# Five changes of order in the second half of a fused two-layer kernel

## The chip, the cores and the metric

The kernel runs on one core of one Trainium2 chip. The metric is the device time of one execution in microseconds (us); the number given for a kernel is the median of its runs. TensorE is also called PE, VectorE DVE, ScalarE ACT, GpSimd POOL and SyncE SP; PEld is TensorE's loading of weights.

## The reference

Two layers act on 2048 tokens of width 128, in float32. Layer 0 is a scan followed by attention and a soft mixture of 8 experts; it takes about the first 950 us and the change does not touch it. Layer 1, cut to what matters here:

```python
xn = layernorm(x)
# recurrent branch
h   = rmsnorm(xn) * w_norm
u, z = split(h @ W_in.T);  u = silu(u)              # 256 + 256 columns
lam = sigmoid(u @ W_dt.T + b_dt)
s_t = lam_t * s_(t-1) + (1 - lam_t) * u_t           # scan over the 2048 tokens
s   = xn + (s * silu(z)) @ W_out.T
# sparse experts: 16 experts, the best 2 of each token
w   = top2(softmax(xn @ Wr + br)), rescaled to sum 1
y_e = layernorm((silu(xn @ W1[e]) * (xn @ W3[e])) @ W2[e]) * gamma[e] + beta[e]
x   = x + s * silu(sum over the 2 experts of w * y_e)
```

## The kernel before, in words

Each engine has its own program, written out by hand; engines meet only in semaphores (`wait_ge`, `then_inc`), and each engine runs its program strictly in the written order. Tokens lie in 16 tiles of 128 rows (`T`), and in 4 chunks of 4 tiles (`C`, 512 tokens each; `LATE` is the last chunk).

**From layer 0 to the router.** VectorE makes the third layernorm chunk by chunk: `third_stats` gives the variance, ScalarE takes its root (`root(3, c)`), `third_apply` writes `xn2`. ScalarE scales the tiles for the RMS norm (`scale_tiles2`, L915), in one run of 12 tiles for the first three chunks, with the last chunk's root after the eighth of them. TensorE transposes both (`turn_norm` for `xn2`, `turn_scaled` for the scaled tiles), each chunk when its four tiles are there, and makes the router's logits. VectorE subtracts the row maximum (L1315), ScalarE takes the exponential (L941) and VectorE finds the two best experts and writes `mask` (L1335). ScalarE loads a table of functions ahead of an operation that needs another than the one in place (`ACT_TABLE_LOAD`); copies and plain scalings run under any table.

**From the mask to the slots.** TensorE counts the mask (`count`, L1888), makes W (the second half of u, L1876), then eight products M of 512 tokens each for `lam` (the step sizes, L1901), then R (`find_slots`, L1915: 32 small products that say which token stands in which slot), then eight products Z. The results go round the eight PSUM banks in the order of `SECOND_MM`. VectorE meanwhile writes R's inputs (`in_tile`, `of_tile`) and names each tile's expert (`name_experts`); then `place_tokens` reads R and writes `token` and `dest`, the rows that POOL's indirect transfers use. After it VectorE runs the scan, `recur(0)` and `recur(1)`; `recur` waits for all eight M.

**The tiles of the experts.** The 4096 token-expert pairs, sorted by expert, fill up to 47 tiles (`NT`) of 128 slots. For tile n:

- POOL gathers its rows (`gather_slots`, L699), up to 4 tiles ahead; SP loads its expert's weights, also up to 4 ahead (512 KB each, L598).
- TensorE transposes the rows (`turn_slots`, L1946), ScalarE copies them out (`copy_slots`, L965); one PSUM bank (`XB`) serves all, so a tile's transpose waits for the copy of the one before.
- TensorE makes the hidden products (`hidden_slots`, L1955), ScalarE their SiLU (`gate_slots`, L971), VectorE the product (`multiply`, L1433), TensorE the output (`outputs`, L1965). `hidden_slots(n)` waits for `multiply(n - 2)`.
- VectorE takes the output with its statistics (`take_output`).

The three first tiles are transposed ahead of the first hidden product, and in the loop tile n + 3 is turned in step n. During steps 2 to 5 TensorE also makes the recurrent branch's output (`states_out`, L1934).

**The groups.** `GROUPS` puts the tiles into eleven groups of four (the last is 40 to 43), then 44 and 45, then 46. After a group's last tile ScalarE takes the roots of its variances (`roots`, L976) and VectorE finishes the group (`finish_outputs`: a reciprocal and one product for each tile, L1461), on which POOL's scatters wait (`scatter_outputs`, L706, one transfer for each tile). `LAG` says how many steps after its last tile a group's roots come; `finish_outputs` came one step later still. When all 47 tiles are scattered, SP and ACT load the rows back (L478), and the rest is elementwise.

Of the kernel before, what the change touches and what calls it, by code (L numbers as in the profile page):

```python
# [42 lines left out]

NT = (2 * N + (P - 1) * E1) // P
GROUPS = [*(range(i, i + 4) for i in range(0, NT - 3, 4)), range(NT - 3, NT - 1), range(NT - 1, NT)]
LAG = [2] * (len(GROUPS) - 4) + [1] * 2 + [0] * 2
XT, RING = 4, 16
INNER = 2 * P

# [25 lines left out]
ROWS_W = _at  # L75
W_IN = 2 * F1
W_RING = 4
PICK = 32


# [59 lines left out]
def build(nc, x, mats, cols, rows, b2, gains, pick, tri, ones, w1, w2, w_in, w_out, out):  # L140
    with ExitStack() as ctx:
# [133 lines left out]
        def row(name):  # L275
# [150 lines left out]
        SECOND_BANK = Steps(A=C, L=1, B=C, U=C, K=1, W=C, M=2 * C, R=1, Z=2 * C)  # L426
        SECOND_MM = Order(("A", 0), ("A", 1), ("A", 2), ("B", 0), ("B", 1), ("A", 3), ("B", 2), ("L", 0),
                          ("U", 0), ("U", 1), ("U", 2), ("B", 3), ("U", 3), ("K", 0), *(("W", c) for c in range(C)),
                          *(("M", i) for i in range(2 * C)), ("R", 0), *(("Z", i) for i in range(2 * C)),
                          *(("Y", c) for c in range(C)))  # L430
        SECOND_ACT = Steps(A=C, B=C, U=C, W=C, M=2 * C, Z=2 * C)
        SECOND_DVE = Steps(L=1, K=1, R=1, Y=C)
# [287 lines left out]
        def _(act):  # L720
# [206 lines left out]
            silu_sum(LATE)  # L927
            act.wait_ge(norm3, LATE * TC)
            act.wait_ge(rms_inv, 1)
            scale_tiles2(0, 2 * TC)  # L930
            root(3, LATE)
            scale_tiles2(2 * TC, LATE * TC)
            copy_turned2(LATE)
            root_means(1)
            for c in range(LATE):
                gain_turned2(c)
            act.wait_ge(norm3, T)
            act.wait_ge(rms_inv, 2)
            scale_tiles2(LATE * TC, T)
            act.wait_ge(route_exp, 1)  # L940
            nc.scalar.activation(rp[:, :, :], rp[:, :, :], ACT.Exp).then_inc(route_exp, 1)  # L941
            gain_turned2(LATE)
            for j in range(2):
                for c in range(C):
# [30 lines left out]
                at = slice(GROUPS[i][0] % RING, GROUPS[i][-1] % RING + 1)  # L975
                nc.scalar.activation(y_rstd[:, at], y_rstd[:, at], ACT.Sqrt).then_inc(y_std, 1)  # L976

            for n in range(3):
                copy_slots(n)
            gate_slots(0)  # L980
            for n in range(NT):
                if n + 1 < NT:
                    gate_slots(n + 1)
                if n + 3 < NT:
                    copy_slots(n + 3)
                for i, group in enumerate(GROUPS):
                    if n == min(group[-1] + max(LAG[i], 1), NT - 1):
                        roots(i)
            nc.scalar.activation(table_set[:, :], table_set[:, :], ACT.Silu)
            act.wait_ge(s_gated, C)  # L990
# [19 lines left out]
        def _(dve):  # L1010
# [460 lines left out]
            for n in range(NT):  # L1471
                if 3 <= n < 3 + C:
                    take_states(n - 3)
                if n + 1 < NT:
                    multiply(n + 1)
                if n > 0:
                    take_output(n - 1)
                if n < C:
                    gate_states(n)
                if n == 3 + C:  # L1480
                    dve.wait_ge(second_dve, SECOND_DVE.n("Y"))
                    dve.nop().then_inc(s_gated, C)
                for i, group in enumerate(GROUPS):
                    if n == group[-1] + LAG[i] + 1:
                        finish_outputs(i)
            take_output(NT - 1)
            finish_outputs(len(GROUPS) - 1)
# [25 lines left out]
        def _(pe):  # L1513
# [327 lines left out]
            def fill_second(step, c, mms):  # L1841
                mms(second_bank(step, c)).then_inc(second_mm, 1)
# [49 lines left out]
            for c in range(C):  # L1892
                if c == C - 1:
                    pe.wait_ge(second_act, SECOND_ACT.n("U", 0))
                fill_second("W", c, from_h(1, c))
            for j in range(2):
                for c in range(C):
                    def mms(bank):
                        for i in range(2):
                            at = (i * 2 + j) * P  # L1900
                            last = pe.matmul(bank, mat("wdt")[:, at:at + P], u[i][:, c * CH:(c + 1) * CH],  # L1901
                                             start=(i == 0), stop=(i == 1))
                        return last
                    i = j * C + c
                    if j == 0:
                        pe.wait_ge(second_act, SECOND_ACT.n("W", c))
                    if i == C - 1:
                        pe.wait_ge(second_dve, SECOND_DVE.n("K"))
                    fill_second("M", i, mms)
            def find_slots(bank):  # L1910
                for k in range(2):
                    pe.wait_ge(in_tile_set, k + 1)
                    pe.wait_ge(of_tile_set, k + 1)
                    for t in range(T):
                        last = pe.matmul(bank[:, 0:2 * NT], in_tile[:, k, t, :], of_tile[k][:, t, :],  # L1915
                                         start=(k == 0 and t == 0), stop=(k == 1 and t == T - 1))
                return last
            pe.wait_ge(second_act, SECOND_ACT.n("M", 0))
            fill_second("R", 0, find_slots)
            for j in range(2):  # L1920
                for c in range(C):
                    i = j * C + c
# [47 lines left out]
            pe.wait_ge(second_act, SECOND_ACT.total)  # L1970
            pe.wait_ge(te_set, 1)
            pe.wait_ge(wall_in, 32)
            for n in range(3):
                turn_slots(n)
            hidden_slots(0)
            for n in range(NT):
                if n + 1 < NT:
                    hidden_slots(n + 1)
                if n > 0:
                    outputs(n - 1)  # L1980
                if 2 <= n < 2 + C:
                    states_out(n - 2)
                if n + 3 < NT:
                    turn_slots(n + 3)
            outputs(NT - 1)


# [65 lines left out]
```

## Time and profile before

| | us |
|---|---|
| Median of 3 runs | 1188.43 |
| Lowest and highest run | 1186.72, 1189.18 |
| The profiled execution | 1186.79 |
| Its span, first to last instruction | 1184.9 |
| PE, DVE, ACT, POOL busy | 1101.9, 909.5, 815.4, 346.9 |

The profile is of one execution; all times of day below are us from its span's start. Between 948 and 1014 us the engines hand work to each other one step at a time; from there to 1148 us TensorE works on the tiles without a pause; the rest is the end.

### The profile page before, as it was taken

What the parts mean: (1) busy time and instruction counts of PE and PEld (TensorE: products, weight loads), DVE (VectorE), ACT (ScalarE), POOL (GpSimd) and SP (SyncE); (2) the same over time, 40 slices, a digit from 0 to 9 for tenths busy, and PEclk for the clock granted to TensorE, in tenths of its full rate; (3) what the DMA queues carried; (4) which work ended last, traced back from release to release, by engine and by line L of the source; (5) the groups of instructions that cost most, each with busy time, mean ns of one, the idle gap of its engine ahead of it and who ended that gap; (6) DMA issues with size and microseconds to landing.
All of it is one profiled execution on the core that took longest, in us unless ns stands there. A gap on an engine that the chain in (4) does not pass through costs nothing.

```text
span 1184.9 us, 19441 instructions
## 1 busy us (share of the span) xinstructions
PE 1101.9 (93%) x6337; PEld 447.5 (38%) x6337; DVE 909.5 (77%) x1413; ACT 815.4 (69%) x1512; POOL 346.9 (29%) x852
## 2 busy tenths in 40 slices
PE   5979999999999999999999999999999979899990
PEld 2412222222222222222222244444444444799990
DVE  3689999999999999999999954433334878756664
ACT  2668888888888888888888864433334565255553
POOL 0476653234222242222322212000000001556752
PEclk9879999999999999999999999999999979899995
DMA  3313321032200322100201026000000001467754
GB/s 113 139 32 80 89 73 53 29 94 51 55 29 29 87 59 51 42 29 29 69 30 39 29 73 263 9 27 19 18 18 18 19 19 66 137 196 241 231 162 122
DMA packets 65496, 87.87 MB, mean 74 GB/s; under 512 B 28579, under 2 KB 39819, under 8 KB 64883
## 3 DMA queue, kind: packets, MB, share of 16 engines
q1 hardware_dynamic: 52434, 70.94, 18.8%
q0 software_dynamic: 10208, 13.45, 4.9%
q10 hardware_dynamic: 2758, 2.28, 0.7%
q8 instruction: 51, 0.84, 0.3%
q14 instruction: 45, 0.36, 0.1%
HBM read 60.83 MB, written 25.76 MB: 73 GB/s over the span
## 4 chain that ended last, share of the span: by engine, by line
PE 39%; issue 33%; POOL 20%; DVE 3%; ACT 2%; DMA 1%; POOLq 0%; DVEq 0%; ACTq 0%; SPq 0%
PE PS L1764 9%; PE PS L1754 9%; PE PS L1955 7%; POOL neg_m L640 6%; POOL big L453 4%; PE PS L1965 3%; POOL big L471 2%; PE PS L1901 1%; DVE mx L1076 1%; PE PS L1529 1%; POOL m_rest L646 1%; POOL m_cols L645 1%; POOL m_cols L647 1%; POOL m_rest L648 1%; POOL m_cols L649 1%
## 5 line engine op out<-in xcount | busy, mean ns | idle before, releaser
L1076 DVE TENSOR_REDUCE mx<-PS 128x1 f32<-128x1024 f32 x512 | 594.1, 1212 | 19.6 <-PE PS L1601 9.1
L1616 PE MATMUL PS<-big 59*128 59x512 bf16 x1024 | 294.6, 387 | 9.1 <-DMA big<-m_dram 2.4
L1601 PE MATMUL PS<-big 56*128 56x512 bf16 x1024 | 201.8, 385 | 16.6 <-DVE mx L1076 8.7
L811 ACT ACTIVATE xn<-PS 128x512 f32<-128x512 f32 x340 | 185.7, 604 | 27.4 <-PE PS L1616 27.4
L811 ACT ACTIVATE ctx_sb<-PS 128x512 f32<-128x512 f32 x344 | 187.8, 604 | 23.8 <-PE PS L1616 23.7
L811 ACT ACTIVATE xnT<-PS 128x512 f32<-128x512 f32 x340 | 185.6, 605 | 21.6 <-PE PS L1616 21.6
L1616 PEld LDWEIGHTS PS<-big 59*128 59x128 bf16 x1024 | 72.6, 94 | 325.5 <-ACT ctx_sb L811 98.6
L640 POOL TENSOR_SCALAR neg_m<-mx 128x1 f32<-128x1 f32 x256 | 68.9, 288 | 372.0 <-DVE mx L1076 372.0
L1206 DVE TENSOR_TENSOR ctx_sb<-big,PS 128x512 f32<-128x512 f32 x128 | 87.8, 686 | 116.4 <-PE PS L1764 70.4
L863 ACT ACTIVATE big<-PS,col_sb 128x512 f32<-128x512 f32 x128 | 87.8, 687 | 123.2 <-PE PS L1754 113.1
L699 POOL DMA_INDIRECT late<-xn_dram,gate_p x47 | 54.0, 1150 | 315.8 <-DVE gate_p L1407 277.2
L1754 PE MATMUL PS<-big,w_bufs 128*128 128x512 f32 x256 | 133.3, 603 | 0.1
L1764 PE MATMUL PS<-ctx_sb,w_bufs 128*128 128x512 f32 x256 | 131.8, 596 | 1.3 <-DVE ctx_sb L1206 1.3
L1601 PEld LDWEIGHTS PS<-big 56*128 56x128 bf16 x1024 | 50.4, 94 | 118.4 <-DVE mx L1076 114.0
L1955 PE MATMUL PS<-big 128*128 128x128 f32 x752 | 93.1, 278 | 0.0
L1628 PE MATMUL PS<-ctx_sb,v_cols 128*32 128x512 f32 x688 | 92.5, 610 | 0.0
L1628 PE MATMUL PS<-xnT,v_cols 128*32 128x512 f32 x680 | 91.2, 609 | 0.0
L1628 PE MATMUL PS<-xn,v_cols 128*32 128x512 f32 x680 | 90.6, 605 | 0.0
L1955 PEld LDWEIGHTS PS<-big 128*128 128x128 f32 x752 | 89.4, 195 | 0.0
L1764 PEld LDWEIGHTS PS<-ctx_sb,w_bufs 128*128 128x128 f32 x256 | 48.5, 191 | 64.0 <-issue 58.4
L1754 PEld LDWEIGHTS PS<-big,w_bufs 128*128 128x128 f32 x256 | 48.5, 192 | 53.9 <-issue 52.1
L1433 DVE TENSOR_TENSOR v_cols<-v_cols,PS 128x512 f32<-128x512 f32 x47 | 32.1, 683 | 40.8 <-ACT v_cols L971 40.8
(250 smaller groups left out, 1031.4 us busy)
## 6 DMA issues: line engine op xcount, KB each, us to landing
big<-in_w_in SPq DMA_DIRECT2D x47, 512.0 KB, 3.8
o_dram<-o_sum SPq DMA_DIRECT2D x64, 256.0 KB, 2.4
big<-parts_dram POOLq DMA_DIRECT2D x42, 128.0 KB, 4.6
w_bufs<-in_w SPq DMA_DIRECT2D x16, 256.0 KB, 2.6
big<-in_w_out SPq DMA_DIRECT2D x2, 2048.0 KB, 10.8
w_bufs<-o_dram SPq DMA_DIRECT2D x3, 1024.0 KB, 5.1
big<-parts_dram SPq DMA_DIRECT2D x62, 48.0 KB
big<-m_dram SPq DMA_DIRECT2D x128, 3.0 KB
```

Of the source, the lines that this page charges most:

```text
L640: ch.did(nc.gpsimd.tensor_scalar(m[:, u:u + 1], mx[:, b % 2, 2 * u:2 * u + 1], mx[:, b % 2, 2 * u + 1:2 * u + 2], -1.0, ALU.max, ALU.mult))
L699: pool.indirect_dma_start(xt[:, n % XT, :], None, xn_dram[:, :], bass.IndirectOffsetOnAxis(ap=token[:, n:n + 1], axis=0))\
L811: nc.scalar.activation(probs[i % SLOTS][:, r, :], PS[:, SB + n % SLOTS, :], ACT.Exp, scale=DH ** -0.5).then_inc(exp_done, 1)
L863: nc.scalar.activation(h_relu[:, f % 2, :], PS[:, HB + f % 2, :], ACT.Relu, bias=col_sb[:, bass.ds(COLS["b1"][0] + e * FT + f, 1)]).then_i ...
L1076: v.tensor_reduce(mx[:, b % 2, 2 * u + half:2 * u + half + 1], PS[:, MB + 2 * half:MB + 2 * half + 2, :].rearrange("p b n -> p (b n)"), AX ...
L1206: v.tensor_tensor(h_wt[:, f, :], h_relu[:, f % 2, :], PS[:, PB + slot, :], ALU.mult)\
L1601: mm = pe.matmul(PS[:, MB + 2 * half + k, :], q_all[rows_of, h, t * P:(t + 1) * P], k_all[rows_of, h, half * CH:(half + 1) * CH], start=Tr ...
L1616: pe.matmul(PS[:, SB + n % SLOTS, :], k_all[rows_of, h, at:at + P], q_all[rows_of, h, qc * CH:(qc + 1) * CH], start=True, stop=True).then_ ...
L1628: mm = pe.matmul(PS[VW * r:VW * (r + 1), PVB, :], v_cols[:, at:at + VW], probs[i % SLOTS][:, r, :], start=(s == 0), stop=(s == TC - 1))
L1754: pe.matmul(PS[:, HB + f % 2, :], w1_buf[:, par, f * P:(f + 1) * P], x1T[:, c * CH:(c + 1) * CH], start=True, stop=True).then_inc(h_mm, 1)
L1764: pe.matmul(PS[:, c, :], w2_buf[:, par, f * P:(f + 1) * P], h_wt[:, f, :], start=(isinstance(e, int) and e == 0 and f == 0), stop=last and ...
L1955: mm = pe.matmul(PS[:, b + n % 2, f:f + P], w_ring[:, n % W_RING, w + f:w + f + P], xtT[:, n % 4, :], start=True, stop=True)
```

## The change

- *Last groups' finish.* `finish_outputs` is placed by a list of its own. For all groups but one the step stays as it was; the group of tiles 40 to 43 is finished in step 44 instead of 45, right after `take_output(43)` and ahead of `multiply(45 + 1)`. The roots on ScalarE stay where they were.
- *First tile's inner products.* Only tile 0 is transposed ahead of `hidden_slots(0)`; tile 1 comes behind it, tile 2 in step 0, tile 3 in step 1, tiles 4 and 5 in step 2, and from step 3 on tile n + 3 as before. ScalarE's copies follow the same order.
- *Slot products ahead of the last step sizes.* R stands between the seventh and the eighth M.
- *Third norm's root.* ScalarE takes the last chunk's root after four scaled tiles instead of eight.
- *Router's exponential.* ScalarE takes it ahead of the last chunk's four scalings instead of behind them.

```diff
-LAG = [2] * (len(GROUPS) - 4) + [1] * 2 + [0] * 2
+LAG = [2] * (len(GROUPS) - 4) + [1] * 4
+FINISH = [3] * (len(GROUPS) - 4) + [2] + [1] * 3
+TURNS = [(2,), (3,), (4, 5), *((n + 3,) if n + 3 < NT else () for n in range(3, NT))]
...
-                          *(("M", i) for i in range(2 * C)), ("R", 0), *(("Z", i) for i in range(2 * C)),
+                          *(("M", i) for i in range(2 * C - 1)), ("R", 0), ("M", 2 * C - 1),
+                          *(("Z", i) for i in range(2 * C)),
...
-            scale_tiles2(0, 2 * TC)
+            scale_tiles2(0, TC)
             root(3, LATE)
-            scale_tiles2(2 * TC, LATE * TC)
+            scale_tiles2(TC, LATE * TC)
...
+            act.wait_ge(route_exp, 1)
+            nc.scalar.activation(rp[:, :, :], rp[:, :, :], ACT.Exp).then_inc(route_exp, 1)
             act.wait_ge(norm3, T)
             act.wait_ge(rms_inv, 2)
             scale_tiles2(LATE * TC, T)
-            act.wait_ge(route_exp, 1)
-            nc.scalar.activation(rp[:, :, :], rp[:, :, :], ACT.Exp).then_inc(route_exp, 1)
...
-            for n in range(3):
-                copy_slots(n)
+            copy_slots(0)
             gate_slots(0)
+            copy_slots(1)
             for n in range(NT):
                 if n + 1 < NT:
                     gate_slots(n + 1)
-                if n + 3 < NT:
-                    copy_slots(n + 3)
+                for turned in TURNS[n]:
+                    copy_slots(turned)
...
-                    if n == group[-1] + LAG[i] + 1:
+                    if n == group[-1] + FINISH[i]:
                         finish_outputs(i)
...
+                    if j * C + c == 2 * C - 1:
+                        pe.wait_ge(second_act, SECOND_ACT.n("M", 0))
+                        fill_second("R", 0, find_slots)
...
-            for n in range(3):
-                turn_slots(n)
+            turn_slots(0)
             hidden_slots(0)
+            turn_slots(1)
...
-                if n + 3 < NT:
-                    turn_slots(n + 3)
+                for turned in TURNS[n]:
+                    turn_slots(turned)
```

## Rows read from the trace of the kernel before

**Rows 1.** Chain of waits, 948 to 981 us: start, length, what.

```profile
961.77 2.34 ACT ctx_sb L915 x8
...
970.67 1.15 ACT ctx_sb L915 x4
...
971.85 1.28 ACT L941
```

**Rows 2.** VectorE in order of time, 940 to 1020 us: start, length, [idle before].

```profile
964.57 0.17 DVE L1022 TENSOR_SCALAR rstd<-moments 128x4 f32<-128x4 f32 x1
...
971.73 0.42 DVE L1315 TENSOR_TENSOR w_bufs<-w_bufs,rs 128x256 f32<-128x256 f32 x1
...
996.49 0.43 DVE L1381 TENSOR_SCALAR o_sum<-o_sum,col_sb 128x752 bf16<-128x752 bf16 x1
```

**Rows 3.** TensorE in order of time, 940 to 1020 us.

```profile
967.12 1.09 PE L1732 MATMUL PS<-mat_sb,xn 128*128 128x128 f32 x4 [1.85 <-DVE xn L1031]
...
980.51 0.40 PE L1888 MATMUL PS<-mask,tri_bf 128*128 128x256 bf16 x1 [1.80 <-DVE mask L1335]
...
980.91 4.82 PE L1876 MATMUL PS<-xnT,mat_sb 128*128 128x512 f32 x8
...
999.30 0.86 PE L1915 MATMUL PS<-late,v_cols 128*128 128x94 bf16 x16
...
1000.70 7.10 PE L1876 MATMUL PS<-xnT,mat_sb 128*128 128x512 f32 x16
1009.28 0.30 PE L1946 MATMUL PS<-mat_sb,late 128*128 128x128 f32 x1 [1.49 <-DMA late<-xn_dram,gate_p]
...
1013.96 5.42 PE L1955 MATMUL PS<-big 128*128 128x128 f32 x32
```

**Rows 4.** VectorE in order of time, 998 to 1048 us.

```profile
1000.89 0.26 DVE L1399 COPY den<-PS 128x94 f32<-128x94 f32 x1 [1.73 <-PE PS L1915]
...
1011.45 4.42 DVE L1394 TENSOR_TENSOR_SCAN ctx_sb<-ctx_sb,xcT 128x2048 f32<-128x2048 f32 x1
```

**Rows 5.** POOL in order of time, 998 to 1048 us.

```profile
1003.43 2.31 POOL L699 DMA_INDIRECT late<-xn_dram,gate_p  x1 [277.20 <-DVE gate_p L1407]
...
1012.53 4.09 POOL L699 DMA_INDIRECT late<-xn_dram,gate_p  x1 [0.30 <-issue]
```

**Rows 6.** ScalarE in order of time, 998 to 1048 us.

```profile
1007.83 0.60 ACT L958 ACTIVATE big<-PS 128x512 f32<-128x512 f32 x1 [0.26 <-PE PS L1876]
```

**Rows 7.** ScalarE's groups, 1013 to 1150 us: busy us, mean ns | idle before.

```profile
L971 ACT ACTIVATE v_cols<-PS 128x512 f32<-128x512 f32 x46 | 27.5, 597 | 47.8 <-PE PS L1955 47.7
...
L965 ACT COPY big<-PS 128x128 f32<-128x128 f32 x45 | 11.9, 265 | 22.3 <-PE PS L1946 22.3
```

**Rows 8.** Chain of waits in the tiles' loop, 1005 to 1030 us.

```profile
1024.96 1.79 PE PS L1934 x16
...
1026.86 1.79 PE PS L1955 x16
1028.64 0.89 PE PS L1965 x8
```

**Rows 9.** Stretches: length, busy PE, PEld, DVE, ACT, POOL, clock, DMA, GB/s.

```profile
952.00:956.00 4.00, 2.67 (x11) 1.31 (x11) 3.90 (x17) 1.49 (x2) 0.00 (x0) 1.00 0.00 0
1007.00:1011.00 4.00, 1.09 (x3) 0.14 (x1) 4.00 (x2) 1.43 (x3) 3.69 (x2) 0.96 0.24 89
```

**Rows 10.** ScalarE in order of time, 1134 to 1185 us.

```profile
1150.88 0.20 ACT L976 ACTIVATE y_rstd<-y_rstd 128x4 f32<-128x4 f32 x1 [0.58 <-DVE y_rstd L1450]
```

**Rows 11.** VectorE in order of time, 1134 to 1185 us.

```profile
1153.03 0.69 DVE L1433 TENSOR_TENSOR v_cols<-v_cols,PS 128x512 f32<-128x512 f32 x1 [2.18 <-ACT v_cols L971]
...
1155.01 1.14 DVE L1461 SCALAR_TENSOR_TENSOR xnT<-xnT,y_rstd,big 128x128 f32<-128x128 f32 x4
```

**Rows 12.** POOL in order of time, 1134 to 1185 us.

```profile
1156.42 0.97 POOL L706 DMA_INDIRECT yt_dram<-xnT,gate_p  x1 [6.19 <-DVE xnT L1461]
...
1164.07 0.97 POOL L706 DMA_INDIRECT yt_dram<-xnT,gate_p  x1 [0.30 <-issue]
```

More of the change, by code:

```diff
@@ L983, in _ @@
                     gate_slots(n + 1)
-                if n + 3 < NT:
-                    copy_slots(n + 3)
+                for turned in TURNS[n]:
+                    copy_slots(turned)
                 for i, group in enumerate(GROUPS):
-                    if n == min(group[-1] + max(LAG[i], 1), NT - 1):
+                    if n == min(group[-1] + LAG[i], NT - 1):
                         roots(i)
@@ L1895, in _, with find_slots @@
                 fill_second("W", c, from_h(1, c))
+            def find_slots(bank):
+                for k in range(2):
+                    pe.wait_ge(in_tile_set, k + 1)
+                    pe.wait_ge(of_tile_set, k + 1)
+                    for t in range(T):
+                        last = pe.matmul(bank[:, 0:2 * NT], in_tile[:, k, t, :], of_tile[k][:, t, :],
+                                         start=(k == 0 and t == 0), stop=(k == 1 and t == T - 1))
+                return last
             for j in range(2):
                 for c in range(C):
+                    if j * C + c == 2 * C - 1:
+                        pe.wait_ge(second_act, SECOND_ACT.n("M", 0))
+                        fill_second("R", 0, find_slots)
                     def mms(bank):
@@ L1909, in _ @@
                     fill_second("M", i, mms)
[L1910 to L1919, printed above, removed]
             for j in range(2):
```

## The prediction

> **What bounds the kernel now.** I read first the chain of waits from 940 us to the end, then the four engines in order of time round each edit, then stretches for the clock. Three stretches matter, each with another bound.
>
> *Router to slots (961 to 1001).* The chain goes ScalarE, TensorE, VectorE in turn. The reader is to see that the exponential's table load starts only at 971.85, behind four scalings that begin at 970.67 [rows 1], although its input is written at 971.73 + 0.42 = 972.15 [rows 2]; that TensorE waits 1.80 us for the mask and then runs W, M, R and Z without a stop [rows 3]; and that VectorE idles 1.73 us until R is there [rows 4]: nothing but R holds the slots.
>
> *First tiles (1001 to 1027).* Z is done at 1007.80, tile 0 is turned at 1009.28, and the first hidden product comes at 1013.96 [rows 3], because all three first tiles are turned ahead of it and POOL's gathers come slowly: 2.31 us for the first, 4.09 for the fourth, where an unhindered indirect transfer takes 0.97 [rows 5, 12]. From 1013.96 to 1148 TensorE has no gap, so what is won ahead of the loop moves the loop whole.
>
> *The end.* POOL's last seven scatters run back to back from 1156.42 to 1164.07, one each (1164.07 - 1156.42) / 6 = 1.275 us [rows 12]; the rest follows them. They wait for the group of tiles 40 to 43, whose root was there at 1150.88 + 0.20 = 1151.08 [rows 10], while VectorE stood for 2.18 us at multiply(46), 1153.03, and finished the group behind it with products from 1155.01 to 1156.15 [rows 11].
>
> **The change part by part.** No instruction is added; DMAs are not reordered, but weight loads start with the tile names and gathers with the slots, so both move.
>
> *Router's exponential.* The load takes 1.28 us (971.85 to its use at 973.13) [rows 1]. It can start at 970.67, ends at 971.95, and the exponential then waits for 972.15 instead of 973.13: **-0.97** for all of VectorE's chain to the mask. The four scalings that it passes start at about 972.6 instead of 970.67, take 1.15 and end at 973.8. Behind them come one chunk's transposes, a copy and the last U, by these rows some 0.9 + 0.6 + 0.9, so 976.2, which must be done when the mask arrives, 980.5 - 0.97: the cover is 3 us, and without it each us late would cost one. Behind the mask everything shifts by 0.97, if the clock allows: W takes 4.82 us [rows 3], where half an M (see the slot products) for each of four would be 3.4 and twice that 6.8: part of it runs at 1.2 GHz after TensorE's wait. If the low stretch ends at the same moment, half of 0.97 is lost (-0.5); if the shorter wait keeps the clock up, W gives 1.4 more (-2.4). I take -0.97, the shift without either.
>
> *Third norm's root.* Four of eight scalings in 2.34 us [rows 1] end at 962.95; a load of 1.28 ends at 964.23; the variance comes at 964.57 + 0.17 = 964.74 [rows 2]. So the root moves from 965.4 to 964.8 and the normed last chunk from 966.98 to 966.4. But the scalings of chunk 1, which TensorE takes first, now end at 964.9 + 1.2 = 966.15, and their four transposes, 0.9 by the rate of the 1.09 row, end at 967.1; the last chunk's are turned at 967.12 now [rows 3]. What is won at the root is late again in the queue: **0** (between +0.1 and -0.45, the latter at the full clock).
>
> *Slot products.* Eight M take (999.30 - (980.91 + 4.82)) / 8 = 1.70 each [rows 3]. R goes ahead by one M. Its inputs are ready at 996.92 [rows 2], R would start at 999.30 - 1.70 = 997.60 in times of now, and VectorE is free at 1000.89 - 1.73 = 999.16, R's end: **-1.70** for `token`, -2.67 with the exponential. The eighth M ends where R ended, so Z does not move, `recur(0)` finds it when `place_tokens` is done, and the scan moves with the slots: its end from 1011.45 + 4.42 = 1015.87 [rows 4] to 1013.2. The eighth sigmoid comes 1.4 later on ScalarE and delays the first SiLUs of Z, which catch up, since each takes 0.60 and TensorE gives one in 0.89 (7.10 / 8) [rows 3, 6].
>
> *First tile's inner products.* With the -2.67 tile 0's rows would be there at 1006.61; TensorE waits for the last SiLU of Z as well, 1007.83 + 0.60 - 0.97 = 1007.46 [rows 6], and that is late next. So the turn is at 1007.5, the copy and the handovers take 0.7 (0.30, then 0.27 [rows 3, 7]), and the first hidden product starts at 1008.2 instead of 1013.96. It does not keep all of that. `copy_slots(1)` now stands behind `gate_slots(0)` on ScalarE, and behind it TensorE's next tile: a SiLU of 0.597, a copy of 0.265 [rows 7] and two handovers, about 1.0 us of idle TensorE. A tile takes 1.79, an output 0.89, `states_out` 1.79, a turn 0.11 (1026.86 - 1024.96 - 1.79) [rows 8]. The walk: tile 0 from 1008.2 to 1010.0; tile 1 from 1011.0 to 1012.8; tile 2 needs the copy at 1013.8 and `multiply(0)`, which waits for the scan's end and takes 0.69 [rows 11], 1013.9, so from 1014.0 to 1015.8; output to 1016.7; turn and copy 0.7; tile 3 from 1017.3 to 1019.1; output and states to 1021.8; tiles 4 and 5 turned with a copy between, 0.75; the fifth tile's products at 1022.55. Now it is 1013.96 + 5.26 for two tiles (half of it at the low clock) + 2 x (1.79 + 0.89) + 1.79 + 3 x 0.11 = 1026.70. From there both orders are the same: **-4.15** for the loop. Without the slot products' 1.70, multiply(0) would hold tile 2 to 1015.7 and it would be -2.5.
>
> *Last groups' finish.* VectorE now waits for the root after `take_output(43)`; queued behind it are multiply(46) and `take_output(44)`, on which the last outputs wait. The root is there at 1151.08; a reciprocal (0.17, as the small operations of [rows 2]) and two handovers of about 0.1 later the four products take 1.14 and end at 1152.57, ahead of 1153.03 where multiply(46) gets its SiLU anyway: the cover is 0.5 us. The scatters start 0.27 later, 1152.83, against 1156.42: -3.59. Seven at 1.275 put the last at 1160.48. Its group must be finished by then. VectorE has `take_output(45)`, a finish of two, `take_output(46)` and a finish of one left, from 1154.7 instead of 1156.15: two outputs at 0.95 (1153.72 to the finish at 1154.66), two roots of 0.20 with 0.3 of handovers, two reciprocals with 0.35, three products at 0.3, and some 0.5 twice for what VectorE's queue does between; 5.5, an estimate, so 1160.2. **-3.55**; were POOL kept by that last finish, -3.0.
>
> *Sum*: -4.15 - 3.55 = -7.7 on the profiled execution's 1186.79, 1179.1. That execution lies 1.64 under the median of the runs shown and at their lower edge; I take the sum from the median, 1188.43: **1180.8**.
>
> **The rivals.**
>
> *The clock falls in the new gaps.* While it waited for the gathers TensorE was busy 1.09 of 4 us, and afterwards ran at 1.2 GHz (the 5.42 row of [rows 3]); at 952 to 956 it was busy 2.67 of 4 and stayed at 2.4 [rows 9]. In the new order it is busy 5.7 of the 9 us from 1007 to 1016, near the second share, which speaks for staying. If it falls, one tile takes 1.7 more: 1182.5; two, 1184.2.
>
> *The gather is held longer.* The fourth gather ended 0.75 after the second scan (1016.62 against 1015.87), gather 0 came through in 2.31 [rows 4, 5]. In the new order gathers and scan shift alike, which speaks against a change. Were gather 0 caught by the first scan, as the fourth is by the second, its rows come 4.42 later, tile 0 turns at 1011.0, 3.5 behind my walk: 1184.3. The Trainium skill ("SBUF — State Buffer", section "SBUF: two separate sides") says that VectorE and GpSimd lock a shared pair of ports for a whole instruction, and the 4.09 agrees with it. By it the winner is who starts first, and that is VectorE, as now.
>
> *The clock stays up at W.* -1.4 more: 1179.4.
>
> *The end gives nothing.* If the root comes 0.5 or more later than computed, multiply(46) and the last outputs shift with it, and the last group holds POOL: 1184.4 at worst.
>
> *Slower: the clock stays down through the first four tiles.* Each burst of products ends in a gap, and now two tiles at the low clock needed 5.26. Tiles 1 to 3 at 1.2 GHz cost 3 x 1.7, two outputs 1.8, the states 1.8: +8.7 against -7.7, 1189.4, and with W all at the low clock (+2) 1191.4. It decides once TensorE does not rise before the fifth tile. The Trainium skill ("TensorE: Matmul & The Clock Gate", section "HAM oscillation — how this bites in real kernels") describes such a kernel, where each burst between waits starts cold again. Its waits are longer than its bursts; here the gaps are 1.0 against 1.79, which speaks against it.
>
> **How the numbers follow.** Forecast 0.60 (1179.8 to 1182); clock falls 0.17; gather held 0.06; clock up at W 0.07; end without gain 0.04; slower 0.06, half of it within 0.2%. The range 1178.4 to 1184.5 takes in the four middle cases' main times and leaves the deep clock case and a start better than all bounds outside. A measurement of this kernel tells about 0.2% (2.4 us) from no change. Faster: all but the slower case and 0.02 of falling clock, 0.92; same 0.05; slower 0.03.
>
> **What would show it.** Right: the exponential about 1 us earlier against its logits; 32 small products ahead of the last M; the first hidden product some 0.7 after the last SiLU of Z, with gaps of about 1 us behind tiles 0 and 1 and a full clock; the scatters of 40 to 43 about 3.6 us earlier against tile 46. Wrong: a low clock from 1010 on, gather 0 longer than 2.5 us, multiply(46) behind the finish, or a root that still holds the last chunk.

## The result, and the profile after

| | before | after |
|---|---|---|
| Median | 1187.65 (7 runs) | 1182.01 (7 runs) |
| Lowest and highest | 1186.72, 1189.18 | 1179.81, 1183.98 |
| Profiled execution, its span | 1186.79, 1184.9 | 1181.53, 1179.7 |
| PE, DVE, ACT, POOL busy | 1101.9, 909.5, 815.4, 346.9 | 1101.7, 909.8, 814.9, 347.7 |

The ratio of after to before is 0.9947, 95% interval [0.9929, 0.9964]: faster by 5.6 us at the medians, by 6.3 by the ratio. 1180.8 was forecast, 7.7 less than before. The busy times differ by less than 1 us; it is waits that went.

ScalarE of the kernel after (start, length, line, operation, [idle before <- what ended it]; lines are before's plus 3). The table load at 972.88 now comes ahead of the four scalings, which start at 974.50 behind the exponential [rows 1]; the last SiLU of Z ends at 1009.76 [rows 6]; the root of tiles 40 to 43 is there at 1149.92 [rows 10].

```profile
972.88 1.28 ACT L941 ACT_TABLE_LOAD   x1
974.17 0.42 ACT L941 ACTIVATE w_bufs<-w_bufs 128x256 f32<-128x256 f32 x1
974.50 1.26 ACT L918 ACTIVATE ctx_sb<-xn,rms 128x128 f32<-128x128 f32 x4
...
1009.16 0.60 ACT L961 ACTIVATE big<-PS 128x512 f32<-128x512 f32 x1 [0.26 <-PE PS L1879]
...
1149.71 0.21 ACT L979 ACTIVATE y_rstd<-y_rstd 128x4 f32<-128x4 f32 x1 [0.58 <-DVE y_rstd L1453]
```

TensorE of the same kernel, the stretch of [rows 3]. R (998.91 to 1000.47) lies ahead of the eighth M. The last chunk of the third norm is turned at 969.34, behind four transposes of chunk 1 (968.43) that wait 2.10 for their scalings. Tile 0 is turned at 1010.03, its products follow at 1010.78 with no other turn between, tiles 1 and 2 wait 0.83 and 0.78 for their copies, and a tile takes 1.86 (the next turn's start less its own). L1960 at 1025.47 is the fifth tile.

```profile
968.43 1.12 PE L1735 MATMUL PS<-mat_sb,ctx_sb 128*128 128x128 f32 x4 [2.10 <-ACT ctx_sb L918]
969.34 1.06 PE L1735 MATMUL PS<-mat_sb,xn 128*128 128x128 f32 x4
...
981.77 5.30 PE L1879 MATMUL PS<-xnT,mat_sb 128*128 128x512 f32 x8
986.90 1.02 PE L1916 MATMUL PS<-sT,mat_sb 128*128 128x512 f32 x2
...
998.91 0.86 PE L1904 MATMUL PS<-late,v_cols 128*128 128x94 bf16 x16
999.61 0.86 PE L1904 MATMUL PS<-o_sum,v_cols 128*128 128x94 bf16 x16
1000.31 1.09 PE L1916 MATMUL PS<-sT,mat_sb 128*128 128x512 f32 x2
...
1010.03 0.30 PE L1951 MATMUL PS<-mat_sb,late 128*128 128x128 f32 x1 [0.91 <-DMA late<-xn_dram,gate_p]
1010.78 2.02 PE L1960 MATMUL PS<-big 128*128 128x128 f32 x16 [0.45 <-ACT big L968]
1012.64 0.27 PE L1951 MATMUL PS<-mat_sb,late 128*128 128x128 f32 x1
1013.74 2.02 PE L1960 MATMUL PS<-big 128*128 128x128 f32 x16 [0.83 <-ACT big L968]
...
1016.65 2.02 PE L1960 MATMUL PS<-big 128*128 128x128 f32 x16 [0.78 <-ACT big L968]
...
1025.47 2.01 PE L1960 MATMUL PS<-big 128*128 128x128 f32 x16
```

Stretches of the same kernel (length, busy PE, PEld, DVE, ACT, POOL, granted clock, DMA share, GB/s): the granted clock holds 1.00, its 2.4 GHz level, through the gaps.

```profile
1011.00:1015.00 4.00, 3.17 (x28) 2.96 (x28) 3.97 (x2) 0.75 (x2) 3.69 (x2) 1.00 0.21 41
1015.00:1019.00 4.00, 3.22 (x29) 3.01 (x29) 3.16 (x5) 1.05 (x3) 3.39 (x3) 1.00 0.72 239
```

VectorE at the end of the same kernel, then POOL: gathers 0 and 3, and the first and the last of the seven scatters. The group of tiles 40 to 43 is finished ahead of multiply(46) (L1436 at 1151.93, which still waits 0.51 for its SiLU), and the seven scatters run from 1151.69 in the old rhythm [rows 11, 12].

```profile
1149.95 0.18 DVE L1459 RECIPROCAL y_rstd<-y_rstd 128x4 f32<-128x4 f32 x1 [0.27 <-ACT y_rstd L979]
1150.28 1.14 DVE L1464 SCALAR_TENSOR_TENSOR xnT<-xnT,y_rstd,big 128x128 f32<-128x128 f32 x4
1151.93 0.69 DVE L1436 TENSOR_TENSOR v_cols<-v_cols,PS 128x512 f32<-128x512 f32 x1 [0.51 <-ACT v_cols L974]
```

```profile
1003.04 2.51 POOL L702 DMA_INDIRECT late<-xn_dram,gate_p  x1 [274.34 <-DVE gate_p L1410]
...
1012.36 4.09 POOL L702 DMA_INDIRECT late<-xn_dram,gate_p  x1 [0.30 <-issue]
...
1151.69 0.96 POOL L709 DMA_INDIRECT yt_dram<-xnT,gate_p  x1 [2.62 <-DVE xnT L1464]
...
1159.34 0.97 POOL L709 DMA_INDIRECT yt_dram<-xnT,gate_p  x1 [0.30 <-issue]
```

**Where the time went.** Stage by stage one compares from a fixed point ahead of the change: the first of ScalarE's scalings of the third norm, 961.67 before and 963.91 after. From there VectorE's last sum ends after 220.51 before and 213.11 after: -7.40. The execution of after that was profiled came 2.24 late to that point, which hides part of it.

### The profile page after: what moved, and what is told of

The parts are those of the page before. It is cut to its first block, busy times and chain, and to the rows that moved or that the text cites. A ratio compares the mean times of both kernels' runs of the same rounds, so it can differ in the third digit from the quotient of the medians.

```text
span 1179.7 us, 19442 instructions
## 1 busy us (share of the span) xinstructions
PE 1101.7 (93%) x6337; PEld 446.2 (38%) x6337; DVE 909.8 (77%) x1413; ACT 814.9 (69%) x1512; POOL 347.7 (29%) x852
## 4 chain that ended last, share of the span: by engine, by line
PE 39%; issue 34%; POOL 19%; DVE 4%; DMA 2%; ACT 2%; POOLq 0%; SPq 0%; ACTq 0%; DVEq 0%
PE PS L1767 9%; PE PS L1757 9%; PE PS L1960 7%; POOL neg_m L643 6%; POOL big L456 4%; PE PS L1970 3%; POOL big L474 2%; PE PS L1532 1%; DVE mx L1079 1%; POOL m_cols L648 1%; POOL m_rest L649 1%; POOL m_cols L650 1%; POOL m_rest L651 1%; POOL m_cols L652 1%; PE PS L1916 1%
## 5 line engine op out<-in xcount | busy, mean ns | idle before, releaser
L1960 PE MATMUL PS<-big 128*128 128x128 f32 x752 | 92.0, 275 | 2.5 <-ACT big L968 2.1
L1960 PEld LDWEIGHTS PS<-big 128*128 128x128 f32 x752 | 87.7, 192 | 3.2 <-issue 3.2
L456 POOL DMA_DIRECT2D big<-parts_dram x90 | 51.5, 606 | 40.7 <-DMA parts_dram<-big 40.4
```

Source lines behind the costliest of these rows:

```text
L456: eng.dma_start(q_all[rows_of, h, FIRST], parts_dram[0, a, h * DH:(h + 1) * DH, FIRST].partition_broadcast(times))\
L1960: mm = pe.matmul(PS[:, b + n % 2, f:f + P], w_ring[:, n % W_RING, w + f:w + f + P], xtT[:, n % 4, :], start=True, stop=True)
```

## The experiments

Theory 1: the five steps work as predicted, and the rest of the difference is what executions differ by in the first part, whatever the kernel. The rivals: the change slows the part ahead of it (Theory 2), or single steps give more or less than their terms. The columns behind the third are starts in each kernel's own profiled execution, counted in us from its first scaling: VectorE's writing of `mask` and its last write of `token` in `place_tokens`, TensorE's products of tile 0 and of tile 4 (the fifth), and POOL's last scatter. The ratios are to runs of before made beside each kernel, whose medians lie between 1187.27 and 1189.49.

| kernel | median | ratio [95%] | first scaling at | mask | token | 1st tile | 5th tile | last scatter |
|---|---|---|---|---|---|---|---|---|
| before | 1187.65 | | 961.67 | 18.35 | 40.71 | 52.28 | 65.02 | 202.40 |
| after | 1182.01 | 0.9947 [0.9929, 0.9964] | 963.91 | 17.15 | 38.09 | 46.87 | 61.56 | 195.44 |
| e1 after again | 1180.72 | 0.9942 [0.9923, 0.9961] | 962.20 | 17.35 | 37.67 | 46.34 | 61.03 | 194.91 |
| e2 finish alone | 1184.11 | 0.9963 [0.9944, 0.9982] | 962.85 | 18.34 | 40.70 | 52.42 | 65.09 | 198.89 |
| e3 R behind M | 1184.71 | 0.9971 [0.9956, 0.9986] | 961.93 | 17.35 | 38.31 | 47.17 | 63.08 | 196.95 |
| e4 three turns first | 1182.87 | 0.9953 [0.9935, 0.9972] | 962.75 | 18.15 | 39.03 | 50.93 | 64.45 | 198.25 |
| e5 before again | 1190.05 | one run | 965.27 | 18.72 | 41.02 | 52.71 | 65.36 | 202.72 |
| e6 exponential behind | 1182.67 | 0.9958 [0.9939, 0.9977] | 963.00 | 18.30 | 38.62 | 47.61 | 63.59 | 197.46 |
| e7 root late | 1180.59 | 0.9936 [0.9915, 0.9957] | 962.88 | 17.40 | 37.72 | 46.56 | 61.25 | 195.12 |
| e8 turns inside, loads held | 1180.32 | 0.9938 [0.9916, 0.9961] | 962.33 | 17.35 | 37.67 | 45.18 | 60.70 | 194.50 |
| e9 loads held longer | 1184.03 | 0.9969 [0.9953, 0.9986] | 963.34 | 17.14 | 38.08 | 46.67 | 62.66 | 196.47 |
| e10 loads held only | 1182.00 | 0.9956 [0.9938, 0.9973] | 961.85 | 17.34 | 37.65 | 45.17 | 64.23 | 198.10 |
| e11 e9, scan halved | 1180.97 | 0.9952 [0.9930, 0.9974] | 967.18 | 18.34 | 38.66 | 46.18 | 61.65 | 195.65 |
| e12 turns inside, scan halved | 1180.13 | 0.9926 [0.9904, 0.9949] | 964.39 | 17.14 | 38.08 | 46.67 | 60.22 | 194.23 |

**e1, e5: both kernels unchanged.**

> The changed kernel once more. Theory 1: between the first scaling of the third norm (L918) and the end it is 7.4 us shorter than before, and where the first profile entered that stretch 2.2 us later (963.91 against 961.67) this came from the first 150 us and differs from execution to execution; so the median of more runs lies 5 to 8 us under before, and the first scaling of this profile stands anywhere from 960 to 966. Theory 2: the changed programs slow the stretch ahead of the edits by about 2 us; then the first scaling stands at 963.5 or later again and the gain stays at 5 to 6 us.

> The kernel before once more, for its stretches. Theory 1: from the first scaling of the third norm (L915) to VectorE's last sum it takes 220.5 us again, within 1 us, while the first scaling stands anywhere from 960 to 966. Theory 2: the first scaling stands at 961.7 again, and only the changed kernels differ there.

The kernel after comes to the first scaling at 963.91 and 962.20, before at 961.67 and 965.27: the spread is as large within a kernel as between them, so Theory 2 falls. From the first scaling to VectorE's last sum e5 takes 220.21, within the 1 us expected of before's 220.51, and e1 212.35, 8.2 less than before; the difference is -8.0 at the medians (1180.72 against 1188.74), -6.9 by the ratio. e1 also shows a rival of the prediction at work, the clock that stays up at W. Its TensorE, 3.60 us for the eight products that took 5.30, and the stretch at W in after, then in e1, with granted clocks of 0.50 and 1.00:

```profile
980.03 0.28 PE L1891 MATMUL PS<-mask,tri_bf 128*128 128x256 bf16 x1 [1.30 <-DVE mask L1338]
...
980.26 3.60 PE L1879 MATMUL PS<-xnT,mat_sb 128*128 128x512 f32 x8
983.70 1.02 PE L1916 MATMUL PS<-sT,mat_sb 128*128 128x512 f32 x2
...
1007.79 0.30 PE L1951 MATMUL PS<-mat_sb,late 128*128 128x128 f32 x1 [1.86 <-DMA late<-xn_dram,gate_p]
```

```profile
982.00:985.00 3.00, 3.00 (x4) 1.04 (x4) 2.76 (x8) 0.60 (x1) 0.00 (x0) 0.50 0.00 0
```

```profile
980.26:983.70 3.44, 3.44 (x11) 1.53 (x9) 2.96 (x9) 2.46 (x5) 0.00 (x0) 1.00 0.00 0
```

M starts 1.49 earlier than in after, but only 0.53 of it reaches the first tile: TensorE stands 1.86 us before the turn, for gather 0's rows.

**e2: the last groups' finish alone.**

```diff
-LAG = [2] * (len(GROUPS) - 4) + [1] * 2 + [0] * 2
+LAG = [2] * (len(GROUPS) - 4) + [1] * 4
+FINISH = [3] * (len(GROUPS) - 4) + [2] + [1] * 3
...
-                    if n == group[-1] + LAG[i] + 1:
+                    if n == group[-1] + FINISH[i]:
```

> Before with the finish of tiles 40 to 43 one step earlier as its only edit. Theory 1: the four scatters start 3.6 us earlier against tile 46, seven of them run back to back, and the time falls by 3.5 us to about 1184. Rival: the wait for the root holds multiply(46) and the last outputs, the last group holds POOL, and less than 2 us are left.

Everything up to the fifth tile is as before (65.09 against 65.02), and the last scatter is 3.51 earlier; -4.6 at the medians, whose interval holds that. The term stands by itself.

**e3: R behind the eighth M again.**

```diff
-            *(("M", i) for i in range(2 * C - 1)), ("R", 0), ("M", 2 * C - 1),
+            *(("M", i) for i in range(2 * C)), ("R", 0),
...
```

> The changed kernel with the slot products behind the eighth M again. Theory 1: token, the gathers and the end of the scan come 1.7 us later, multiply(0) holds tile 2, and the fifth tile's products start 1.5 to 1.7 us later against the first scaling: 1.6 us slower than the changed kernel. Rival: the last SiLU of Z holds tile 0 anyway and the edit is worth under 0.4 us.

Here W ran at the full clock, as in e1. `token` is only 0.64 later than in e1, not the 1.7 of theory 1, since with W quick VectorE's own chain (naming the experts) holds the copy of R in e1. The fifth tile is 2.05 later all the same, for a reason that neither theory has. TensorE of e3, and a stretch of its first tile:

```profile
1008.35 0.30 PE L1948 MATMUL PS<-mat_sb,late 128*128 128x128 f32 x1 [2.71 <-DMA late<-xn_dram,gate_p]
1009.10 3.24 PE L1957 MATMUL PS<-big 128*128 128x128 f32 x16 [0.45 <-ACT big L967]
1012.14 0.42 PE L1948 MATMUL PS<-mat_sb,late 128*128 128x128 f32 x1
```

```profile
1010.00:1013.00 3.00, 2.56 (x12) 2.15 (x11) 3.00 (x1) 0.62 (x2) 2.69 (x2) 0.50 0.10 22
```

TensorE waits 2.71 us for rows instead of 1.86, the granted clock falls to 0.50, its 1.2 GHz level, in tile 0, and that tile takes 3.04 (1012.14 less 1009.10) instead of 1.86. A step that is 0.8 later costs 1.2 more in clock. The median of e3 is 4.0 over that of e1, twice the 2.05; the profiled execution was the fastest of its twelve, and what the others lost on top is not shown.

**e6: the exponential behind the scalings again.**

```diff
-            act.wait_ge(route_exp, 1)
-            nc.scalar.activation(rp[:, :, :], rp[:, :, :], ACT.Exp).then_inc(route_exp, 1)
             act.wait_ge(norm3, T)
             act.wait_ge(rms_inv, 2)
             scale_tiles2(LATE * TC, T)
+            act.wait_ge(route_exp, 1)
+            nc.scalar.activation(rp[:, :, :], rp[:, :, :], ACT.Exp).then_inc(route_exp, 1)
```

> The changed kernel with the exponential behind the last chunk's scalings again. Theory 1: the mask comes 1.0 to 1.2 us later against the first scaling, and so do token and the fifth tile, up to what the clock at W gives or takes (1.5 either way): 1.0 slower than the changed kernel. Rival: W runs half of what is gained at 1.2 GHz, 0.5 or less.

Mask and `token` are 0.95 later than in e1, the term of the prediction. The first tile is 1.27 later and the fifth 2.56, where theory 1 had 1.0 with W at the same clock; the last 1.3 is the same fall of the clock, granted at 0.50 from 1011.1 to 1014.5 (tile 0 takes 3.11):

```profile
1009.86 0.30 PE L1951 MATMUL PS<-mat_sb,late 128*128 128x128 f32 x1 [2.19 <-DMA late<-xn_dram,gate_p]
1010.60 3.32 PE L1960 MATMUL PS<-big 128*128 128x128 f32 x16 [0.45 <-ACT big L968]
1013.71 0.42 PE L1951 MATMUL PS<-mat_sb,late 128*128 128x128 f32 x1
```

**e7: the third norm's root behind eight scalings again.**

```diff
-            scale_tiles2(0, TC)
+            scale_tiles2(0, 2 * TC)
             root(3, LATE)
-            scale_tiles2(TC, LATE * TC)
+            scale_tiles2(2 * TC, LATE * TC)
```

> The changed kernel with the third norm's last root behind eight scalings again. Theory 1: root 0.6 later, the last chunk turned at the same moment against the first scaling, nothing lost. Rival: the root's 0.6 us arrives at the logits and the mask, 0.6 slower.

The root comes 3.74 behind the first scaling instead of 3.10, and the last chunk is turned at 5.46 instead of 5.43: nothing, as predicted. In after the queue ahead of that turn is just what the prediction named: four transposes of chunk 1, late by the scalings that now follow the root. The fifth tile moves by 0.2, and the median (1180.59 against 1180.72) not beyond what it tells.

**e4: all three turns ahead of the first products again.**

> The changed kernel with three tiles turned ahead of the first hidden product again. Theory 1: the first product starts 2.7 us later, but tiles 0 to 3 follow without gaps, TensorE waits long enough to run the first two at 1.2 GHz, and the fifth tile starts only about 0.9 us later than in the changed kernel; were the clock kept up, 0.9 us earlier. Rival: the order is worth most of the 5 us by which the first product moved, 3 us or more.

The clock of this execution fell sooner (granted 0.50 from 961.0 to 962.4, ahead of the first scaling, where e1 still had 1.00), and the last chunk is turned at 6.44, not 5.43; so I count from `token`: to the fifth tile 25.42, against 23.47 in after and 23.36 in e1. The new order of turns is worth 2.0 here, between the 0.9 of theory 1 and the rival's 3, and the rows show by what: the third turn waits for the third gather, and then two tiles take 6.05, at a granted 0.50, instead of 3.72 and two gaps.

```profile
1010.34 0.30 PE L1950 MATMUL PS<-mat_sb,late 128*128 128x128 f32 x1 [1.43 <-DMA late<-xn_dram,gate_p]
...
1013.41 0.48 PE L1950 MATMUL PS<-mat_sb,late 128*128 128x128 f32 x1 [1.82 <-DMA late<-xn_dram,gate_p]
1013.68 6.21 PE L1959 MATMUL PS<-big 128*128 128x128 f32 x32
1019.73 0.27 PE L1950 MATMUL PS<-mat_sb,late 128*128 128x128 f32 x1
```

**e8, e9, e10: why gather 0's rows are late.** In after its issue ends at 1005.55, Z's last SiLU at 1009.76, and tile 0 is turned at 1010.03, 0.27 later; in e1 it is 1.23 later (1006.56, then 1007.79). The four weight loads of 512 KB issued from 1000.98 on run meanwhile. All three experiments hold the loads of tiles 2 and 3 back, on SP; e8 and e9 also move turns (ScalarE's copies move with them, which the cut below leaves out).

```diff
+                if n == 2:
+                    sp.wait_ge(xt_in[0], 16)     # e8;  xt_in[1] in e9 and e10
...
+            # e8: turns 1 and 2 in the middle of the tile before, on TensorE
+                    if b == H3B and n < 2:
+                        turn_slots(n + 1)
+            # e8 and e9: turns 3 and 4 ahead of outputs(0) and outputs(1)
+                if 1 <= n < 3:
+                    turn_slots(n + 2)
```

> The changed kernel with tiles 1 and 2 turned in the middle of the hidden products of the tile before, tiles 3 and 4 turned ahead of outputs(0) and outputs(1), and the weight loads of tiles 2 and 3 held until tile 0's rows are there. Theory 1: no gap behind tile 0, but multiply(0) behind the scan's end still holds tile 2; the gaps behind outputs(0) and tile 4's turn go; the fifth tile starts 1.4 us earlier against the first scaling, and tile 0 up to 1.1 earlier where its rows came after Z. Rival: the gaps alone held TensorE, and the fifth tile starts 2.9 earlier.

> The changed kernel with one thing more: the weight loads of tiles 2 and 3 are issued only when the rows of gather 1 are in, and the turns of tiles 3 and 4 stand on TensorE ahead of the output products of tiles 0 and 1 (turns 1 and 2 as in the changed kernel). Counted from the first scaling of the third norm, the run of the changed kernel beside e2 had the first token's number at 37.67, gather 0's rows and Z's last SiLU at 45.6 and 44.36, the first inner product at 46.34 and the fifth tile's at 61.03. Theory 1 (gather 0 is late because it runs behind the queued weight loads; the first tile's turn is then set by Z's last SiLU, 44.4, and tiles 3 and 4 no longer wait for the turn that stands behind an output product): first product at about 45.2, fifth tile at 59.5 to 60.0, median about 1.2 us under that of the changed kernel of the same call or of e1 (1180.72). Rival (loads held longer come late themselves, and gather 1 still waits for VectorE's scan): tile 2 waits for its weights, fifth tile at 61 or later, median as e1 or up to 1 us over it.

> The changed kernel with the weight loads of tiles 2 and 3 issued only when the rows of gather 1 are in; all turns as in the changed kernel. Theory 1: the first product comes 1.1 us earlier than in the changed kernel (45.2 after the first scaling against 46.34), but tiles 3 and 4 still wait for turns that stand behind output products, and multiply(0) behind the scan's end holds tile 2, so the fifth tile's start moves by 0.3 us at most (60.7 to 61.0). Rival (the transfers are what holds the first five tiles): all of the 1.1 us arrives at the fifth tile, 59.9.

The cause is confirmed: in all three the rows are there in time and tile 0 is turned 0.05 us after Z's last SiLU, with a first tile at 45.17 and 45.18 in e10 and e8 (e1 46.34); in e9 W ran at the low clock, and Z alone holds it to 46.67. But the collision only moves on. TensorE of e8, of e9 and of e10, the wait that takes its place in each (e10 with its first turn ahead of it), and the granted clock behind e10's wait:

```profile
1011.18 0.48 PE L1956 MATMUL PS<-mat_sb,late 128*128 128x128 f32 x1 [2.54 <-DMA late<-xn_dram,gate_p]
```

```profile
1019.37 0.33 PE L1955 MATMUL PS<-mat_sb,late 128*128 128x128 f32 x1 [1.46 <-DMA late<-xn_dram,gate_p]
```

```profile
1006.24 0.33 PE L1953 MATMUL PS<-mat_sb,late 128*128 128x128 f32 x1 [0.69 <-ACT big L963]
...
1018.32 0.33 PE L1953 MATMUL PS<-mat_sb,late 128*128 128x128 f32 x1 [1.70 <-DMA late<-xn_dram,gate_p]
```

```profile
1020.20:1023.40 3.20, 3.20 (x17) 3.20 (x17) 0.69 (x1) 0.60 (x1) 0.19 (x1) 0.50 0.10 29
```

In e8 it is gather 1, in e9 and e10 gather 3 that lies behind the held loads: issued by 1015.86 in e9, turned 3.5 us later. e8 keeps 0.33 of its 1.2 at the fifth tile, and neither the 1.4 of theory 1 nor the 2.9 of its rival came; e9 and e10 lose 1.1 (against after, with W at the same clock) and 3.2 (against e1). Part of this is the clock again: it falls to 0.50 behind the waits of e8 and e10, sixteen products of e8 take 2.97 (1011.45 to 1014.42) instead of 1.86, and of e10's 3.2 the wait gives 1.6 (its fourth tile starts at 57.21 instead of 55.63) and the clock the other 1.6. My theory for e9 and e10 expected -1.0 to -1.5 and -0.3; it fell, and the rival that held loads come late had it, though by a gather and not by the weights themselves.

**e11, e12: the second scan in halves, multiply(0) between them.** e11 is e9 with it; e12 has e8's turns and no held load.

```diff
+                half = C * CH // 2
+                ch.step(v.tensor_tensor_scan(lam[j][:, 0:half], lam[j][:, 0:half], u[j][:, 0:half], 0.0,
+                                             ALU.mult, ALU.subtract))
+                multiply(0)
+                v.tensor_tensor_scan(lam[j][:, half:], lam[j][:, half:], u[j][:, half:], lam[j][:, half - 1:half],
+                                     ALU.mult, ALU.subtract).then_inc(lam_scan, 1)
...
```

> The kernel of e9 with the second scan of VectorE in two halves of 1024 columns and the first tile's product with its gate (multiply(0)) between them. Theory 1 (multiply(0) behind the scan's end, 51.15 after the first scaling, is what holds the third tile at 52.21): third tile at 50.5 to 51.2, fifth tile 0.7 to 1.0 earlier than in e9, median 0.7 to 1.0 under e9. Rival (gather 2 gets its rows only after the scan, and that holds the third tile; or the wait for the gate's SiLU, at about 48.9, and a second start of the scan make the states late): third tile as in e9, median the same or up to 1 us above e9.

> The turns of e8 (turns 1 and 2 in the middle of the previous tile's inner products, turns 3 and 4 ahead of the output products of tiles 0 and 1), weight loads as in the changed kernel (not held), and the second scan in two halves with multiply(0) between them, as in e11. Counted from the first scaling of the third norm, e1 (the changed kernel) had the first five tiles at 46.34, 49.29, 52.21, 55.63 and 61.03; the rows of its gathers 1, 2 and 3 had landed at 46.6, 48.8 and 53.4. Theory 1 (the gaps behind tiles 0 and 1 are the turn and its copy, and with the turns inside, the rows there in time and the scan halved, nothing holds them): first tile as in e1, then 48.3, 50.3, 53.5 and 58.5 to 59.3 for the fifth, and the median 1.5 to 2.5 us under e1 (1180.72), at 1178.2 to 1179.2. Rival (the loads' collisions with the gathers only move on to the third and fourth gather, as they did in e9 and e10): turn 3 or 4 waits for rows for 1 us or more, the fifth tile at 60.5 or later and the median as e1.

The clock of e11's execution fell sooner, as e4's did (granted 0.50 from 965.1 to 967.1, ahead of the first scaling), and it is 1.0 late from the last chunk's transposes on; W ran at the full clock. So I count from the mask and against e10, whose first tile stands at the same place (27.84 and 27.83). The third tile is at 33.71 against 34.53, the 0.8 expected; against e9 there is no difference that is the scan's, since there the first tile itself is late and the third follows it by 5.87 in both. Gather 3's issue ends at 32.42 instead of 34.55, and no wait of its turn is marked in the rows. The fifth tile is at 43.31, against 43.68 in e1: -0.4. e12 on TensorE, on VectorE, then gathers 3 and 4 on POOL:

```profile
1011.07 1.13 PE L1972 MATMUL PS<-big 128*128 128x128 f32 x8 [0.45 <-ACT big L968]
...
1012.14 1.95 PE L1972 MATMUL PS<-big 128*128 128x128 f32 x16
1014.33 0.33 PE L1961 MATMUL PS<-mat_sb,late 128*128 128x128 f32 x1 [0.24 <-DMA late<-xn_dram,gate_p]
...
1017.49 0.33 PE L1961 MATMUL PS<-mat_sb,late 128*128 128x128 f32 x1 [0.15 <-DMA late<-xn_dram,gate_p]
1018.46 1.15 PE L1982 MATMUL PS<-big,v_cols 128*128 x8 [0.63 <-issue]
```

```profile
1011.74 2.29 DVE L1409 TENSOR_TENSOR_SCAN ctx_sb<-ctx_sb,xcT 128x1024 f32<-128x1024 f32 x1
1014.07 0.69 DVE L1398 TENSOR_TENSOR v_cols<-v_cols,PS 128x512 f32<-128x512 f32 x1
1014.67 2.34 DVE L1412 TENSOR_TENSOR_SCAN ctx_sb<-ctx_sb,xcT 128x1024 f32<-128x1024 f32 x1
```

```profile
1012.83 1.96 POOL L702 DMA_INDIRECT late<-xn_dram,gate_p  x1 [0.30 <-issue]
1015.09 2.68 POOL L702 DMA_INDIRECT late<-xn_dram,gate_p  x1 [0.31 <-issue]
```

The gaps behind tiles 0 and 1 are gone but for 0.24, and no turn waits longer for rows: the rival falls at the turns, though the median lies nearer to it. W ran at the low clock; against after, which had that too, the second to fourth tiles are 1.2, 1.7 and 1.1 earlier, the fifth 1.34 (60.22 against 61.56). I had expected 1.7 to 2.5 against e1; what is missing goes between the third and fourth tiles, 4.05, where 0.63 of a wait named issue and a turn stand ahead of the output products. Its median, 1180.13, is the lowest of all, but 0.6 under e1, not 1.5 to 2.5, is less than these runs can tell, and the intervals of the ratios 0.9926 and 0.9942 overlap: by the trace it beats the changed kernel, by the medians that is open.

## Why the prediction was right

**Sum and median.** -7.7 was forecast; from the first scaling on it is -7.40 in after and -8.16 in e1, at the medians -5.6 and -8.0. Both ratios' intervals (4.3 to 8.4 us for after, 4.6 to 9.2 for e1) hold 7.7, and the difference between the two medians is within the noise of the runs. I took the sum from the median 1188.43, and not from the profiled execution, 1.64 below: executions of one kernel enter the second half at 961.67 to 965.27, so a sum made in one execution can't be set against another to better than that. (1188.43 less 7.70 is 1180.7.)

**Exponential**, -0.97: the mask came 1.20 earlier in after, 1.00 in e1, and undoing it gives 0.95 back. Of the three cases for W behind it, after comes near the middle value taken (M 0.90 earlier, with W at 5.30), e1 shows the best (M 2.39 earlier, W at 3.60). The middle value is luck: it was to be the shift with nothing lost at W, and it is 1.20 won at the mask less 0.30 lost between mask and M, where W is slower than before.

**Root**, 0: 0.64 earlier at the root, 0.02 at the turn (e7). Right for the reason given.

**Slot products**, -2.67 at `token` with the exponential: -2.62 and, in e1, -3.04. In after the sum has the same luck in it: 1.20 at the mask, 0.30 lost at W, 1.72 by R. The condition that nothing but R holds the slots is true only while W runs slow. When it runs fast, VectorE's naming of the experts is the bound, and R ahead of the last M is worth 0.64 at `token` (e3).

**First tile**, -4.15 at the fifth tile: -3.46 in after, -3.99 in e1. Two parts of the term were mis-sized in after. The turn of tile 0 was to follow Z's last SiLU, 45.83 from the first scaling; it came at 46.12, since I let gather 0's rows follow its end as before, and they came behind the weight loads: these moved up by 1.4 only (the first is issued at 38.51 before, 37.07 in after), the gather by 2.4 (its issue ends at 44.07 and 41.65). And the walk from the first to the fifth tile took 14.69, not 14.35: a tile among waits takes 1.86, not the 1.79 of the packed loop; turn and copy ahead of the fourth and the fifth tile take 0.67 and 0.86, where the walk, 0.1 short in its own sum, had 0.6 and 0.75; and the gaps were 1.10 and 1.05, not 1.0 and 1.2, since tile 2 waited for its copy and not for multiply(0). In e1 the first of the two is larger (the turn comes 1.23 behind the last SiLU), and hidden by W's quicker clock. The clock held through the gaps, so neither the rival of falling clock nor the slower one came. The kernel stands near it, though: in e6 and e3 it fell behind 2.19 and 2.71 us of waiting before the turn, in after, e1 and e7 it held behind 0.91, 1.86 and 2.04. That is why the terms don't add: undoing the exponential and R separately costs 2.56 and 2.05 at the fifth tile, more together than the first five tiles won.

**Last groups' finish**, -3.59 at the scatters and -3.55 at the last: counted from the products of tile 46 the first of the seven scatters starts at 3.77 instead of 7.33 and the last at 11.42 instead of 14.98, -3.56 both. The cover of 0.5 is the 0.51 that multiply(46) still waits; POOL was not kept by the last finish.

**The gather held longer** did not come: gathers 0 and 3 took 2.51 and 4.09, against 2.31 and 4.09 [rows 5]. (2.51 is over the 2.5 named as a sign of being wrong; e1 has 2.31, and it is not what made the rows late.) The halved scan of e12 shows how VectorE holds the transfer: gather 3 ended 0.75 us after the first half, at 1014.78, gather 4 at 1017.77, 0.76 after the second; in after gather 3 ended 0.76 after the whole scan (1016.44 against 1015.69). Gather 1 of after ended at 1009.84, 0.79 after the first scan, while VectorE's next long product ran from 1008.96. So a gather gets through between two instructions of VectorE. The Trainium skill ("SBUF — State Buffer", section "SBUF: two separate sides") has the shared pair of ports locked for a whole instruction, and that agrees.

## What to carry to other kernels

Ahead of a loop without gaps, order the first pass so that the first unit waits only for its own inputs, and look at what the clock does with the wait that is left: here 0.8 us more of waiting cost 2.0 (e3). A transfer that is late behind queued large loads is not helped by holding some of them, if the next small transfer then lies behind those. And compare two executions from a common point just ahead of the change: what lies before it differed by up to 3.6 us within one kernel.

## What the runs showed of the hardware

- The same kernel gave two states of the clock at W. In e1 TensorE was still busy with U shortly before, waited 1.30 us for the mask and made W in 3.60 at a granted clock of 1.00; in after it had finished U sooner, waited 3.16 and made W in 5.30, granted 0.50 from 982 to 985. The wait alone does not decide it: e6 waited 2.22 and kept 1.00, before waited 1.80 and had 0.50 from 980 to 983.
- An indirect gather issued while 512 KB loads run brings its rows late: in e9 the last completion of gather 3 came 3.5 us after its issue's end (1015.86 to 1019.32), that of gather 0, with the loads over at 1005.27, 1.7 us after (1004.98 to 1006.70).
- A table load in the middle of ScalarE's work took 1.28 us and the next operation started 0.01 us behind it (in after 972.88, then 974.17).
